# Re-ordering VectorE's stream in a fused two-layer gated cross-attention and mixture-of-experts kernel: an early zeroing of the values' tile, and four moved steps

## The chip, the cores and the metric

The kernel runs on one core of a Trainium2 chip. The metric is the device time in microseconds of one execution. A core has a matrix engine (TensorE, "PE" in the profile), VectorE ("DVE"), ScalarE ("ACT"), GpSimd ("POOL") and a queue engine (SyncE, "SP"), each with an instruction stream of its own that runs in order; streams meet only at semaphores, which this kernel sets and waits for by hand.

## The reference

The state x is 16 sequences of 128 tokens and 128 features, all in fp32. Two layers, each an attention over a context of 77 keys per sequence followed by an expert block:

```
x = x + tanh(g_xattn[0]) * single_head_attention(layernorm(x), ctx)
x = x + tanh(g_ffn[0])   * moe(layernorm(x), 16 experts, top 4, sigmoid gates, one shared expert)
x = x + tanh(g_xattn[1]) * attention_16_heads_of_8(layernorm(x), ctx, Wq, Wk, Wv, Wo and biases)
x = x + tanh(g_ffn[1])   * moe(layernorm(x), 8 experts, top 2, softmax gates)
# an expert: (silu(x @ Wgate) * (x @ Wup)) @ Wdown, weighted by the token's gate
```

## The kernel before, in words

The 16 sequences are four groups g of four tiles t (128 tokens each); a group's tokens are the 512 columns of most operations. The kernel has four stages, here A (first attention), B (first expert block, object `mB`), C (16-head attention), D (second expert block, object `mD`). All orders are written out by hand, engine by engine.

**Start.** SP issues the loads of x, group by group, between other loads. GpSimd zeroes or fills seven small tiles, signals `built` after `qq` (L332), and goes on to zero `VS` (L333), a staging tile for the values of stage C. VectorE waits for `built` and then for the first group of x, and takes its layer-norm statistics (`norm_statsA`, L1069). GpSimd raises the variance to the power -0.5 (`inv_stdA`), VectorE applies it (`norm_applyA`).

**Stages A to B.** The keys of stage C are computed late in stage A: TensorE makes them for one group (`setup_keys`), ScalarE writes the high part, VectorE the low part (`keys_lo(g)`, L1122, semaphore `k_l`). TensorE waits for `k_l` of 3, which is `keys_lo(2)`, before it enters the expert loop of stage B (L663). `VX`, the tile from which stage C's values are multiplied, holds zeroes outside of the copied blocks; GpSimd clears all of it once (L379), after the square root of group 1 (`inv_std(NG + 2)`, L378) and before it splits the shared expert's second matrix `W2S`.

**Expert blocks.** A group has eight units k. For unit k TensorE makes gate and up parts (`m_up`, three passes of a split fp32 product each, L542), ScalarE applies silu into `sg`, VectorE multiplies by the up part (`m_gated`, L1195), then by the token's expert weights (`m_weighted`, L1200), and TensorE multiplies by the down matrix (`m_down`, L564). TensorE runs `m_up(k + 2)` ahead of `m_down(k)`, and `m_up(k)` waits for `m_gated(k - 2)`. The expert weights come through DRAM: the gates are turned on TensorE (`m_route_T`), copied by ScalarE to `ct`, written to `comb_rows`, and read back, broadcast over partitions, into a ring `CR` of four slots (SP, `weight_rows`, L294). Between the units VectorE also does the next group's layer norm (`norm_apply`, L1054; `norm_lo`, L1063) and its routing: `route_add`, `route_vals`, `route_top` (L1147), `route_pick` (L1154), `route_weights` (L1170). In stage B unit 1 is followed by the shared expert's `hs` product (L1223).

**Stage C.** For tile n, TensorE makes the scores (L689), VectorE takes maxima and subtracts them (`c_max`, `c_center`), ScalarE exponentiates, TensorE transposes the probabilities (L699), ScalarE copies them out, TensorE mixes the values (`c_mix`, L713), VectorE divides by the sums (`c_normalize`, L1346), TensorE turns (`c_turn`, L722) and projects (`c_project`, L727), and VectorE adds to x (`c_final`, L1358). `c_turn(n - 2)` and `c_mix(n - 1)` stand in TensorE's stream in the middle of tile n. In the last group stage D's first routing is laid between the tiles.

Of the kernel before, what the change touches and what calls it, by code (L numbers as in the profile page):

```python
# [79 lines left out]
def flamingo(nc, x, ctxT, ctx, w0, w4, gate_router, w13, w2, up, down, consts, out, comb_rows):  # L80
    with ExitStack() as stack:
# [18 lines left out]
        def sem(name):  # L100
            return stack.enter_context(nc.semaphore(name))
# [9 lines left out]
        VX = sb("VX", [P, 2, NC, P])  # L111
# [105 lines left out]
            "c_sc", "c_mx", "c_sub", "c_exp", "c_tr", "c_ev", "c_pv", "c_rs", "c_norm", "c_ot", "c_otc", "c_wo",  # L217
            "c_fin"))
        vs_zero, vx_rdy, wo_rdy = sem("vs_zero"), sem("vx_rdy"), sem("wo_rdy")
        sh_up, sh_silu, sh_hid, sh_hi, sh_lo = map(sem, ("sh_up", "sh_silu", "sh_hid", "sh_hi", "sh_lo"))  # L220
# [104 lines left out]
        def _(pool):  # L325
# [52 lines left out]
            inv_std(NG + 2)  # L378
            nc.gpsimd.memset(VX[:], 0.0)  # L379
            pool.wait_ge(in_w2, 16)  # L380
# [651 lines left out]
        def _(dve):  # L1032
            V = nc.vector
# [178 lines left out]

            def m_body(m, g, nxt, then=None, stats_of=None, apply_next=True, begun=0):

                for k in range(m.units):
                    if k >= begun:
                        m_gated(m, g, k)
                    m_weighted(m, g, k)
                    if then:
# [27 lines left out]
                if then:  # L1247
                    then(m.units)

            dve.wait_ge(in_x[0], 16)  # L1250
            norm_statsA(1, 0)
# [50 lines left out]
            m = mB  # L1302
            m_gated(m, 0, 0)
            norm_apply(NG + 2, 1)
            keys_lo(2)
            m_gated(m, 0, 1)
# [59 lines left out]
            def c_body(g, last):  # L1366
                for t in range(GB):
# [6 lines left out]
                    if ahead:  # L1374
                        c_max(*divmod(n + 1, GB), 0)
                        c_center(*divmod(n + 1, GB), 0)
                    else:
                        route_weights(mD, 0)
                    if n >= 2:
# [8 lines left out]
                    if t == 1 and last:  # L1388
                        route_add(mD, 0)
                    if t == 2 and last:  # L1390
                        route_top(mD, 0)
                        route_pick(mD, 0)
                    if t == 2 and not last:
# [17 lines left out]
            m = mD  # L1411
            m_gated(m, 0, 0)
            c_final(NG - 1, GB - 2)
            c_normalize(NG - 1, GB - 1)
            c_final(NG - 1, GB - 1)


            norm_apply(3 * NG + 2, 1)
            for g in range(NG - 1):
                m_body(m, g, (3 * NG + g + 2, m, g + 1), stats_of=g + 2 if g + 2 < NG else None,  # L1420
                       begun=0 if g else 1)
            m_body(m, NG - 1, None)
# [55 lines left out]
```

## Time and profile before

| | us |
|---|---|
| median of 3 runs | 310.07 |
| the three runs | 307.72, 310.07, 310.26 |
| the profiled execution, device time | 309.45 |
| its span in the profile | 307.6 |
| TensorE busy in it | 278.5 (91%) |
| VectorE busy | 235.0 (76%) |
| ScalarE busy | 130.8 (43%) |
| GpSimd busy | 87.6 (28%) |

The profiled execution has 1.85 us around its span that the profile does not show. The busy time of TensorE is that of modelled ends, so 91% does not mean that it can't be shortened. The granted clock of TensorE averages 0.988 of full speed.

### The profile page before, as it was taken

Reading aid. Unit: us, or ns where it says so; the run is one execution under the profiler, and the core shown is the slowest. Engines: PE = TensorE matmul, PEld = TensorE weight load, DVE = VectorE, ACT = ScalarE, POOL = GpSimd, SP = SyncE. Lnnn points to the kernel's source line nnn. Section 1 sums busy time; section 2 is a strip of 40 time slices with the busy share of each in tenths; the row PEclk is TensorE's granted clock in tenths of the full one; section 3 lists DMA queues with packets and bytes.
Section 4 is the critical chain, followed back from the end, with each engine's and each line's share of the span. In section 5 each row is a group of like instructions: output and inputs, shape, how many; then the busy total and the mean of one; then the engine's idle time right before and its main releaser. Section 6 shows DMA issues by size and latency. Waiting matters only on the chain.

```text
span 307.6 us, 5453 instructions
## 1 busy us (share of the span) xinstructions
PE 278.5 (91%) x1646; PEld 209.3 (68%) x1646; DVE 235.0 (76%) x660; ACT 130.8 (43%) x275; POOL 87.6 (28%) x162
## 2 busy tenths in 40 slices
PE   6799869988999979969989899899899999999994
PEld 5589547666656646637878788789767676676661
DVE  2887879947888998787977977887568869777572
ACT  1497623242234323276656556464622332422330
POOL 8376130100082041452555654751110100100000
PEclk9999979997999999999999999999999999999999
DMA  6900056163143243000000000000043051430640
GB/s 216 351 39 1 4 199 183 52 211 114 41 140 131 48 148 120 26 0 2 2 1 2 0 2 3 0 2 1 6 155 116 29 210 39 153 107 19 233 145 34
DMA packets 15066, 25.26 MB, mean 82 GB/s; under 512 B 2341, under 2 KB 4339, under 8 KB 14835
## 3 DMA queue, kind: packets, MB, share of 16 engines
q1 hardware_dynamic: 12968, 23.88, 23.8%
q10 hardware_dynamic: 2072, 1.07, 1.3%
q8 instruction: 13, 0.21, 0.3%
q14 instruction: 13, 0.11, 0.1%
HBM read 22.98 MB, written 1.25 MB: 79 GB/s over the span
## 4 chain that ended last, share of the span: by engine, by line
PE 67%; DVE 9%; DMA 8%; ACT 5%; issue 4%; POOL 4%; SPq 2%; POOLq 0%; DVEq 0%; ACTq 0%
PE S L542 24%; PE Ybank L564 15%; PE Ybank L713 9%; DMA CR<-comb_rows 4%; PE bank L699 4%; PE S L689 3%; ACT pt L976 2%; DMA comb_rows<-ct 2%; PE Tb L482 2%; DMA X<-in_x 2%; DVE cmx L1334 1%; SPq L307 1%; PE bank L580 1%; POOL KT L354 1%; DVE xn L1059 1%
## 5 line engine op out<-in xcount | busy, mean ns | idle before, releaser
L861 ACT ACTIVATE sg<-S 128x512 f32<-128x512 f32 x64 | 38.1, 597 | 75.4 <-PE S L542 67.2
L1205 DVE TENSOR_TENSOR hb<-sg,CR 128x512 f32<-128x512 f32 x64 | 44.6, 697 | 15.0 <-issue 5.9
L1198 DVE TENSOR_TENSOR sg<-sg,S 128x512 f32<-128x512 f32 x64 | 43.5, 680 | 3.4 <-PE S L542 2.1
L337 POOL TENSOR_TENSOR rstd<-ve,mhalf 128x4 f32<-128x4 f32 x11 | 11.1, 1011 | 111.5 <-DVE ve L1052 111.5
L713 PE MATMUL Ybank<-VX,pt 128*128 128x128 f32 (+1 forms) x320 | 39.7, 275 | 0.0
L542 PE MATMUL S<-xh,WBH 128*128 128x512 f32 x64 | 34.6, 540 | 5.1 <-DVE kk L1125 2.7
L713 PEld LDWEIGHTS Ybank<-VX,pt 128*128 128x128 f32 (+1 forms) x320 | 37.9, 192 | 0.4
L542 PE MATMUL S<-xh,UPH 128*128 128x512 f32 x64 | 36.1, 564 | 0.0
L564 PE MATMUL Ybank<-hb,downw 128*128 128x512 f32 x64 | 33.0, 599 | 0.4 <-DVE hb L1205 0.4
L564 PE MATMUL Ybank<-hb,W2T 128*128 128x512 f32 x64 | 33.1, 602 | 0.0
L1334 DVE TENSOR_REDUCE cmx<-S 128x8 f32<-128x616 f32 x32 | 25.4, 794 | 4.6 <-PE S L689 4.3
L418 POOL COPY VX<-VS 128x36 f32 (+3 forms) x80 | 13.7, 220 | 47.5 <-PE Ybank L713 39.7
L1342 DVE TENSOR_TENSOR PX<-S,cmx 128x616 f32<-128x616 f32 x32 | 25.6, 799 | 1.1
L966 ACT ACTIVATE PX<-PX 128x616 f32<-128x616 f32 x32 | 22.7, 712 | 8.7 <-DVE PX L1342 8.7
L542 PE MATMUL S<-xl,WBH 128*128 128x512 f32 x64 | 26.0, 405 | 0.0
L542 PE MATMUL S<-xh,WBL 128*128 128x512 f32 x64 | 25.9, 405 | 0.0
L542 PE MATMUL S<-xh,UPL 128*128 128x512 f32 x64 | 25.2, 394 | 0.0
L542 PE MATMUL S<-xl,UPH 128*128 128x512 f32 x64 | 25.0, 391 | 0.0
L976 ACT ACTIVATE pt<-bank 128x512 f32<-128x512 f32 (+1 forms) x32 | 15.7, 490 | 18.1 <-PE bank L699 17.9
L542 PEld LDWEIGHTS S<-xh,WBH 128*128 128x128 f32 x64 | 12.6, 196 | 15.0 <-DVE sg L1198 6.7
L354 POOL TENSOR_TENSOR KT<-kk,CB 128x616 fp32r<-128x616 f32 x16 | 19.7, 1234 | 5.8 <-PE S L689 5.8
L699 PE MATMUL bank<-CB,PX 128*128 128x128 f32 x96 | 16.9, 285 | 3.0 <-ACT pt L976 3.0
(164 smaller groups left out, 502.9 us busy)
## 6 DMA issues: line engine op xcount, KB each, us to landing
CR<-comb_rows SPq DMA_DIRECT2D x64, 128.0 KB, 3.1
CR<-comb_rows SPq DMA_DIRECT2D x32, 256.0 KB, 3.3
w13raw<-in_w SPq DMA_DIRECT2D x1, 1088.0 KB, 11.0
X<-in_x SPq DMA_DIRECT2D x4, 256.0 KB, 6.2
upraw<-in_up SPq DMA_DIRECT2D x4, 256.0 KB, 4.0
out_x<-X SPq DMA_DIRECT2D x4, 256.0 KB, 3.3
cT<-in_ctxT SPq DMA_DIRECT2D x2, 308.0 KB, 5.6
CN<-in_ctx SPq DMA_DIRECT2D x1, 616.0 KB
```

Of the source, the lines that this page charges most:

```text
L354: nc.gpsimd.tensor_tensor(KT[:, par].rearrange("p a (h k) -> p a h k", h=HG), keys, heads, ALU.mult).then_inc(ks_done, 1)
L542: i = mm(dst, wp[:, col:col + P], xp[:, bass.ds(xs, GT)], start=n == 0, stop=n == 2)
L564: mm(Ybank[:, bass.ds(slot(g), GT)], m.wd[:, k, :], hb[:, k % 2, :], start=k == 0, stop=k == m.units - 1, skip_group_check=True).then_inc( ...
L699: i = tr(bP[r][0:w, c % 4 * P:c % 4 * P + P], PX[:, t % 2, chunk_col(c):chunk_col(c) + w], I)
L713: i = mm(bO9[u], pt[0:w, t % 2, c * P:(c + 1) * P], VX[0:w, t % 2, c, :], start=c % CU == 0, stop=c % CU == CU - 1)
L861: A(sg[:, k % 2, :], Gb[k % 2][:], ACT.Silu).then_inc(m.s_done, 1)
L966: A(p, p, ACT.Exp).then_inc(c_exp, 1)
L976: A(pt[:, t % 2, 4 * r * P:4 * r * P + w], bPa[r][:, 0:w], ACT.Copy).then_inc(c_ev, 1)
L1198: V.tensor_tensor(sg[:, k % 2, :], sg[:, k % 2, :], Ub[k % 2][:], ALU.mult).then_inc(m.t2, 1)
L1205: V.tensor_tensor(hb[:, k % 2, :], sg[:, k % 2, :], CR[:, k % RING, :], ALU.mult).then_inc(m.h_done, 1)
L1334: V.tensor_reduce(cmx[:, 2 * u:2 * u + 2, :], pair(u), AX, ALU.max, negate=True).then_inc(c_mx, 1)
L1342: V.tensor_tensor(PX[:, t % 2, u * UK:(u + 1) * UK].rearrange("p (s h k) -> p s h k", s=2, h=HG), pair(u), cmx[:, 2 * u:2 * u + 2, :].unsq ...
```

## The change

VectorE, not GpSimd, zeroes `VX`, as its first instruction of all; GpSimd waits for that at the old place. `keys_lo(2)` stands ahead of `norm_apply` of group 1. In stage C `route_top` and `route_pick` of stage D's first group move from behind tile 14's work to behind `c_normalize` of tile 13 in the next step, right ahead of `route_weights`. At the entry of stage D the first `m_weighted` and the second `m_gated` stand ahead of the last `c_final`, where they stood behind it and behind `norm_apply`; `m_body` gets a parameter to leave the first weighted product out.

```diff
@@ gpsimd
             inv_std(NG + 2)
-            nc.gpsimd.memset(VX[:], 0.0)
+            pool.wait_ge(vx_zero, 1)
             pool.wait_ge(in_w2, 16)
@@ vector
-            def m_body(m, g, nxt, then=None, stats_of=None, apply_next=True, begun=0):
+            def m_body(m, g, nxt, then=None, stats_of=None, apply_next=True, begun=0, weighted=0):
                 for k in range(m.units):
                     if k >= begun:
                         m_gated(m, g, k)
-                    m_weighted(m, g, k)
+                    if k >= weighted:
+                        m_weighted(m, g, k)
@@
+            V.memset(VX[:], 0.0).then_inc(vx_zero, 1)
             dve.wait_ge(in_x[0], 16)
             norm_statsA(1, 0)
@@
             m_gated(m, 0, 0)
+            keys_lo(2)
             norm_apply(NG + 2, 1)
-            keys_lo(2)
             m_gated(m, 0, 1)
@@ c_body
                     if ahead:
                         c_max(*divmod(n + 1, GB), 0)
                         c_center(*divmod(n + 1, GB), 0)
                     else:
+                        route_top(mD, 0)
+                        route_pick(mD, 0)
                         route_weights(mD, 0)
@@
                     if t == 1 and last:
                         route_add(mD, 0)
-                    if t == 2 and last:
-                        route_top(mD, 0)
-                        route_pick(mD, 0)
@@
             m_gated(m, 0, 0)
             c_final(NG - 1, GB - 2)
             c_normalize(NG - 1, GB - 1)
+            m_weighted(m, 0, 0)
+            m_gated(m, 0, 1)
             c_final(NG - 1, GB - 1)
             norm_apply(3 * NG + 2, 1)
             for g in range(NG - 1):
                 m_body(m, g, (3 * NG + g + 2, m, g + 1), stats_of=g + 2 if g + 2 < NG else None,
-                       begun=0 if g else 1)
+                       begun=0 if g else 2, weighted=0 if g else 1)
```

## Rows read from the trace of the kernel before

**Rows 1.** The page: the chain that ended last, shares by engine

```profile
PE 67%; DVE 9%; DMA 8%; ACT 5%; issue 4%; POOL 4%; SPq 2%; POOLq 0%; DVEq 0%; ACTq 0%
```

**Rows 2.** The chain in order of time, 38 to 48 us: start, duration, what

```profile
38.36 2.44 DVE xn L1059 x4
...
41.39 2.92 PE S L542 x6
...
46.47 1.39 PE S L542 x6
```

**Rows 3.** Timeline, first 9 us: start, duration, what, count, idle before and releaser

```profile
2.40 3.70 POOL L333 MEMSET VS<- 128x4320 f32 x1
...
5.00 0.87 DVE L1074 BATCH_NORM_STATS2 st<-X 128x6 f32<-128x128 f32 x4 [5.00 <-DMA X<-in_x]
...
7.24 0.87 DVE L1074 BATCH_NORM_STATS2 st<-X 128x6 f32<-128x128 f32 x4 [0.45 <-DMA X<-in_x]
```

**Rows 4.** Timeline, 37 to 48 us, from stage A into B

```profile
37.77 0.68 DVE L1198 TENSOR_TENSOR sg<-sg,S 128x512 f32<-128x512 f32 x1
...
38.01 2.23 POOL L379 MEMSET VX<- 128x2560 f32 x1
...
41.39 0.79 PE L542 MATMUL S<-xh,WBH 128*128 128x512 f32 x1 [2.67 <-DVE kk L1125]
...
41.86 1.28 DVE L1205 TENSOR_TENSOR hb<-sg,CR 128x512 f32<-128x512 f32 x2
...
45.84 0.68 DVE L1223 TENSOR_TENSOR hs<-hs,bank 64x512 f32<-64x512 f32 x1 [2.25 <-ACT hs L898]
...
46.46 0.69 DVE L1065 TENSOR_TENSOR xl<-Tb,xh 128x512 fp32r<-128x512 f32 x1
...
47.70 0.18 PE L588 MATMUL Tb<-GW,xh 128*128 128x32 f32 x1
```

**Rows 5.** Line 1059's instructions: min, median and max ns, first and last start

```profile
L1059 DVE TENSOR_SCALAR xn<-X,mv,rstd x28: 328/343/1956, 38.4 to 264.5; 128x128 f32<-128x128 f32 x20, 128x128 f32 x8
```

**Rows 6.** The two ring loads issued at 38.5 and 39.1 us (slot 1): their landing

```profile
DMA to landing us min/median/max: 3.1/3.2/3.2
```

**Rows 7.** Stretches: length, each engine's busy time, TensorE's granted clock, DMA

```profile
41.50:42.00 0.50, 0.50 (x2) 0.41 (x3) 0.50 (x2) 0.00 (x0) 0.00 (x0) 0.50 0.66 238
...
73.00:74.00 1.00, 1.00 (x4) 0.89 (x4) 0.42 (x1) 0.00 (x0) 0.00 (x0) 0.50 0.54 193
...
217.00:218.00 1.00, 0.92 (x8) 0.92 (x9) 0.25 (x3) 0.51 (x3) 0.00 (x0) 1.00 0.00 0
```

**Rows 8.** Timeline, 213 to 220 us, the last tiles of stage C

```profile
213.05 2.40 PE L713 MATMUL Ybank<-VX,pt 128*128 128x128 f32 x20
...
215.06 0.39 DVE L1151 MAX8 top<-valsD 128x8 f32<-128x14 f32 x4
...
216.46 0.25 DVE L1352 RECIPROCAL rec<-Ybank 128x16 f32<-128x16 f32 x1
...
217.09 0.33 PE L722 MATMUL Tb<-CB,On 128*128 128x128 f32 x1 [1.20 <-DVE On L1355]
...
218.33 0.29 DVE L1364 TENSOR_TENSOR X<-Tb,X 128x128 f32<-128x128 f32 x1
...
219.24 0.27 PE L594 MATMUL Tb<-CB,combD 128*32 128x128 f32 x1
```

**Rows 9.** Landing of stage D's first ring load (issued at 221.84); of all ring loads

```profile
DMA to landing us min/median/max: 3.4/3.4/3.4
...
DMA to landing us min/median/max: 2.7/3.2/5.2
```

**Rows 10.** Timeline, 225 to 230 us, entry of stage D

```profile
225.12 0.29 DVE L1355 TENSOR_TENSOR On<-Ybank,rec 128x128 f32<-128x128 f32 x1
...
228.20 0.68 DVE L1205 TENSOR_TENSOR hb<-sg,CR 128x512 f32<-128x512 f32 x1
...
229.03 1.10 PE L564 MATMUL Ybank<-hb,downw 128*128 128x512 f32 x2
```

More of the change, by code:

```diff
@@ L218, in flamingo @@
             "c_fin"))
+        vx_zero = sem("vx_zero")
         vs_zero, vx_rdy, wo_rdy = sem("vs_zero"), sem("vx_rdy"), sem("wo_rdy")
```

## The prediction

> **What bounds the kernel now.** I read the page's chain of work first: two thirds of the span are TensorE's own instructions, one behind the other, and a tenth is VectorE's [rows 1]. So only what removes or shortens a wait of TensorE, or of the chain that hands over to it, can count; the reader should look for the places where the chain leaves TensorE. Then the chain in order of time, which shows one such place at 38 us: a `norm_apply` of 2.44 us on VectorE, and TensorE's six passes behind it, 2.92 us where the same six take 1.39 later [rows 2]. Then the timelines around the four edits, and for each idle time the engine that ended it [rows 3, 4, 8, 10].
>
> **The zeroing leaves GpSimd (stage A to B).** The four `xn` instructions of `norm_apply` start at 38.36; the row of their line gives a median of 343 ns and one of 1,956 ns [rows 5]. The long one is the first of the four: it starts inside the GpSimd zeroing, which runs 38.01 + 2.23 = 40.24 [rows 4], and 38.36 + 1.96 = 40.32. It is held until GpSimd has finished. With the zeroing gone, 1.96 - 0.34 = 1.6 us leave VectorE's stream. What comes to stand there on GpSimd is the short split of `W2S`, which could hold the first `xn` by some tenths; I charge 0.1 to 0.2 within the roundings below. The Trainium skill, page "SBUF — State Buffer", section "Who interferes with whom", names this: a VectorE operation in a two-port mode, such as tensor_scalar, and a GpSimd operation exclude each other for the whole instruction, and the later one blocks. By it the `W2S` split, if issued first, would hold `xn` until its own end; the sum stays.
>
> **keys_lo(2) ahead of norm_apply.** TensorE stands idle 2.67 us until 41.39, for `keys_lo(2)` [rows 4]. In the new order that follows the gated product of 37.77 (next start some 0.61 later, 38.4) and takes at most what a 512-column operation takes, 0.69 [rows 4]: done by 39.0. TensorE enters the expert loop at 39.0, 2.4 sooner. I don't count that 2.4, but follow the chain to the next point where both orders meet, the logits of the next group, which begin at 47.70 [rows 4]:
> - VectorE: `norm_apply` to 40.0, second gated product to 40.7, first weighted product to 41.4. The second weighted product needs ring slot 1, whose second half is issued at 39.1 and lands 3.2 later, at 42.3 [rows 6]. Before, it started at 41.86 + 0.6 = 42.5 [rows 4]. So VectorE meets a transfer here, and all its lead shrinks to 0.2. It goes on: product to 42.9, `keys_lo(3)` to 43.4.
> - Then VectorE before stood idle 2.25 us for ScalarE's shared-expert silu, until 45.84 [rows 4], which waited for TensorE. TensorE now makes: 39.0, six passes 1.4 [rows 2], three for the shared expert 0.7, the turn of `xn` about 0.5, to 41.6; so ScalarE has its input at 41.1 and is not behind 43.4 by more than a tenth or two, with three operations of some 0.6 after 41.4. The `hs` product starts at 43.4 to 43.5, 2.4 sooner, and `xl`, before at 46.46, ends at 44.7 rather than 47.15.
> - TensorE: down product at 41.6, six passes by 43.5, then it waits for `xl` until 44.75. Logits at 44.75 rather than 47.70: **2.9 us**. Should the clock fall as before (the granted clock was 0.50, of its two levels 1.2 GHz, right after the idle time [rows 7]) in the first six passes, they take 2.9 instead of 1.4, and TensorE arrives at about 44.8 to 45: hardly a loss, since `xl` ends last.
>
> Does the 2.9 last? VectorE is ahead by 2.4 only, so 0.5 less than TensorE; from here on TensorE sets the pace (its passes follow without idle time in the chain), and I take VectorE's reserve as larger than 0.5. The next group's weights leave for DRAM behind TensorE's turn and come back through the ring; nothing there waits for an absolute time, so the whole lead goes through stage B. Bounds: 1.9 (the `xn` is still long, see the rivals) to 3.6 (with full clock and a slot landing sooner).
>
> **The zeroing comes to VectorE's start.** VectorE has no zeroing in the trace, so I bound it. From 128 to 512 columns two VectorE rows grow from 0.29 [rows 10] to 0.68 [rows 4], 1.02 ns a column, so 2,560 columns cost 2.6 + 0.16 = 2.8 us; at 0.68 / 512 all in, 3.4; GpSimd's own rate gives 2.23. I take 2.8, from rows of the same engine. The Trainium skill, page "VectorE: DVE Perf Modes", section "Zero memsets can be issued as uint32 (trn2)", gives one cycle an element, from which an estimate at its 0.96 GHz is 2.7 us. GpSimd frees VectorE when `VS` starts, 2.40 [rows 3], plus a tenth or two for VectorE's own semaphore steps: the zeroing ends at 5.3 to 5.4, at most 6.0. VectorE's first statistics start at 5.00, but before the second set it is idle 0.45 until the load lands at 7.24 [rows 3]. So an end up to 5.45 is free, and beyond that it costs one for one: **0 to 0.55, taken as 0.1**. GpSimd's wait at the old place is for something done 30 us before: nothing.
>
> **Routing picks in the last tile of stage C.** `route_top` to the end of `route_pick` fill 215.06 to 216.46, and `c_normalize` begins then, although its input, the mix of 213.05 + 2.40 = 215.45, is ready 1.0 sooner; TensorE's turn waits 1.20 us for it, to 217.09 [rows 8]. Reversed, `c_normalize` (0.25 + 0.29 [rows 8, 10]) runs from 215.5, and the turn comes at about 216.1. What is late next: the picks end at 217.4, `route_weights` at about 218.0, `c_final` at 218.3; before, `c_final` began at 218.33 and `m_route_T` at 219.24 [rows 8]. Moved by 1.0, TensorE would reach `m_route_T` at 218.25 and finds `c_final` just done: 0.9 remains. ScalarE's tanh now waits for the picks between two copies and delays a copy by 0.2, which only a mix four microseconds on uses. **Gain 0.9**, bounds 0.5 to 1.0.
>
> **The entry of stage D.** The first weighted product needs the first ring load, issued at 221.84 and landed 3.4 later, at 225.24 [rows 9]; VectorE reaches it at 225.12 + 0.29 = 225.4 [rows 10]. Both move together by 0.9. So it costs 0.6 in a time when VectorE waited for TensorE's last projection, and the gated product too. `norm_apply` comes no later. Then the down product no longer follows a product begun at 228.20, but the turn: it starts at about 228.9 instead of 229.03 [rows 10], and the next passes save some hundredths. **Gain 0.2**, bounds 0.4 and a loss of 1.6 (rivals).
>
> **Sum.** -2.9 + 0.1 - 0.9 - 0.2 = -3.9 against the profiled execution: 309.45 - 3.9 = 305.55 (span 303.7). That execution lies 0.62 below the median of the runs; the median of all four executions shown (307.72, 309.45, 310.07, 310.26) is 309.76, and from that I forecast 305.9.
>
> **Rivals.**
> - *The clock takes part of it back.* TensorE gets a new idle time of 1.2 us (43.5 to 44.75). In stage B an idle time came before a second stretch at 0.50 of the clock, at 73 us; the 1.20 us in stage C was followed by full clock, at 217 us [rows 7, 8]. Should it fall for 3.2 us, 1.6 are lost: -2.3, 307.5. Chance 0.12.
> - *VectorE's zeroing is held at the start by GpSimd's `VS`*, as the `xn` was by `VX`. `VS` ends at 6.10 [rows 3], the zeroing then at 8.9, 3.4 beyond the free 5.45: net -0.5, 309.3. Against it: the statistics of 5.00 ran beside `VS` in 0.87, as the undisturbed ones did at 7.24 [rows 3]. The skill's SBUF section above exempts a VectorE instruction with at most one SBUF input outside the two-port modes, and so lowers this chance. Chance 0.06.
> - *Slower than before*: the same hold, and with it TensorE's clock. It idles 3.4 us longer in stage A, more than the 2.67 that came before the fall to 0.50 [rows 4, 7], and loses 1.6 to slow passes: 3.9 against 5.0, 310.9. It decides from the point where the zeroing ends later than 5.45 + 3.9 = 9.35. Chance 0.05, of which little lies over 1%.
> - *The first ring load of stage D lands late.* At 5.2, the longest landing of a ring load [rows 9], VectorE holds the last `c_final` and `norm_apply` by 1.6: -2.3, 307.5. Chance 0.07.
> - *The long `xn` had another cause* and stays: then only `keys_lo(2)` gains, and the logits come 1.9 sooner: -2.9, 306.9. Chance 0.05.
>
> **How the numbers follow.** The forecast as told has 0.65. Its own spread is the bounds, 304 to 307.5. The range takes in the clock, the late load and half of the hold: 303.8 to 309.2. About 1% (3.1 us) is what a measurement of this kernel can tell from no change. Faster by more: most of the forecast's case and part of the last rival, 0.65; within 1%: the clock, the late load, the hold, and the forecast's lower edge, 0.30; slower by more, 0.05.
>
> **What would show it.** No instruction of line 1059 at 38 us above 0.4; TensorE's wait for `kk` below 0.5 in place of 2.67, and a new one for `xl` of about 1.2 just before the logits; VectorE's wait for ScalarE before `hs` gone and a short one for the ring before the second `hb`. At the start a zeroing of 2.7 to 2.8 on VectorE, and the second statistics still at 7.24. In the last tile of stage C the turn's idle time near 0.2. At the entry of stage D no wait before the first `hb`. The prediction is wrong if the second statistics start late, if the clock reads 0.5 after 44 us, or if the lead of 2.9 at the logits has shrunk where the next group's weights are written.

## The result, and the profile after

The changed kernel takes 303.22 us, the median of 6 runs (302.62 to 303.55); the kernel before took 307.58 beside it (median of 6, 305.13 to 310.26; three of the six are the runs that the forecast was made from). The ratio is 0.987 [0.984, 0.990]: 1.3% faster. The forecast was 305.9 (range 303.8 to 309.2), a gain of 3.9 us or 1.26%. The gain between the medians is 4.4 us, and the time itself lies 0.6 us below the range.

The profiled execution of the changed kernel took 303.55 us (span 301.7, mean granted clock 0.993) against 309.45 (span 307.6, clock 0.988): 5.9 us less, more than the medians differ. The page, first its engines, then the shares of the chain that ended last (compare [rows 1]):

```profile
PE 277.1 (92%) x1646; PEld 208.5 (69%) x1646; DVE 236.2 (78%) x661; ACT 130.8 (43%) x275; POOL 85.5 (28%) x161
...
PE 70%; DVE 8%; DMA 6%; ACT 5%; POOL 4%; issue 4%; SPq 0%; POOLq 0%; DVEq 0%; ACTq 0%
```

TensorE has 70% of the chain instead of 67%: waits went, and its work stayed.

**The start.** Timeline of the changed kernel, first 9 us (compare [rows 3]):

```profile
2.40 3.70 POOL L334 MEMSET VS<- 128x4320 f32 x1
...
3.64 2.19 DVE L1252 MEMSET VX<- 128x2560 f32 x1 [3.64 <-issue]
...
5.75 0.81 DVE L1075 BATCH_NORM_STATS2 st<-X 128x6 f32<-128x128 f32 x4
...
7.39 0.87 DVE L1075 BATCH_NORM_STATS2 st<-X 128x6 f32<-128x128 f32 x4
```

The zeroing's row is 2.19 us long, not 2.8 (how long it holds VectorE, f2 below shows); it starts at 3.64, later than forecast, and ends at 5.83. The first statistics move from 5.00 to 5.75, the second from 7.24 to 7.39. `VS` beside it on GpSimd lasts 3.70, as before.

**Stage A to B.** Timeline of the changed kernel, 37 to 46 us (compare [rows 4]):

```profile
37.91 0.67 DVE L1199 TENSOR_TENSOR sg<-sg,S 128x512 f32<-128x512 f32 x1
...
38.15 0.29 POOL L382 CAST W2S<-W2T 128x128 fp32r<-128x128 f32 x1
...
39.12 0.54 DVE L1126 SCALAR_TENSOR_TENSOR kk<-bank,CB,kk 128x308 fp32r<-128x308 f32 x1 [0.54 <-ACT kk L856]
39.58 1.11 DVE L1060 TENSOR_SCALAR xn<-X,mv,rstd 128x128 f32<-128x128 f32 x4
...
42.33 0.69 DVE L1206 TENSOR_TENSOR hb<-sg,CR 128x512 f32<-128x512 f32 x1 [0.45 <-DMA CR<-comb_rows]
...
43.99 0.68 DVE L1066 TENSOR_TENSOR xl<-Tb,xh 128x512 fp32r<-128x512 f32 x1
...
45.07 0.18 PE L589 MATMUL Tb<-GW,xh 128*128 128x32 f32 x1
```

`norm_apply` fell from 2.53 (2.44 of it in the chain) to 1.11. The second weighted product waits 0.45 for its ring load, the new wait that the prediction named. The logits (the product with `GW`, L588 before, L589 here) start at 45.07 instead of 47.70, 2.63 sooner (forecast 2.9). The wait before `hs` is gone.

The chain in order of time, same kernel (compare [rows 2]), and under it stretches of it: length, busy time of each engine with its instructions, then granted clock, DMA share and GB/s (compare [rows 7]):

```profile
34.91 2.81 PE S L543 x6
38.53 1.40 PE S L543 x6
...
43.84 1.39 PE S L543 x6
```

```profile
36.00:38.00 2.00, 2.00 (x6) 1.46 (x5) 1.81 (x10) 1.11 (x2) 0.82 (x1) 0.50 0.06 16
...
42.00:44.00 2.00, 2.00 (x11) 1.34 (x10) 1.67 (x4) 1.76 (x3) 0.00 (x0) 1.00 0.58 211
72.00:76.00 4.00, 4.00 (x16) 2.63 (x15) 3.55 (x15) 0.69 (x2) 0.00 (x0) 1.00 0.22 77
```

Between 10 and 290 us the clock still falls once, but earlier (34.8 to 38.2 us). The stretch at 0.50 of the kernel before at 71.9 to 75.3 us ([rows 7] has its middle) is not there.

**Stage C's end and the entry of D.** Timeline, 210 to 223 us (compare [rows 8, 10]):

```profile
210.10 0.26 DVE L1355 RECIPROCAL rec<-Ybank 128x16 f32<-128x16 f32 x1 [0.33 <-PE Ybank L714]
...
210.60 0.39 DVE L1152 MAX8 top<-valsD 128x8 f32<-128x14 f32 x4
210.74 0.33 PE L723 MATMUL Tb<-CB,On 128*128 128x128 f32 x1 [0.24 <-DVE On L1358]
...
219.05 0.68 DVE L1206 TENSOR_TENSOR hb<-sg,CR 128x512 f32<-128x512 f32 x1
...
222.63 1.02 PE L565 MATMUL Ybank<-hb,downw 128*128 128x512 f32 x2
```

The turn waits 0.24 instead of 1.20, and the first weighted product of D waits for nothing.

To add up, I cut both profiled executions at events that both have: TensorE's turn that sends group 0's weights off (`m_route_T`), the logits of group 1, the four writes of `comb_rows` in stage B (one for each group, the last three used here), the four in stage D, and the end. Each step is a difference of two starts in a timeline.

| step (us) | before | after | difference | forecast |
|---|---|---|---|---|
| start to the turn | 34.47 | 34.61 | +0.14 | +0.1 |
| turn to logits | 13.23 | 10.46 | -2.77 | -2.9 |
| logits to the write of group 1 | 10.89 | 10.89 | 0 | 0 |
| write of group 1 to that of group 2 | 24.77 | 21.54 | -3.23 | 0 |
| write of group 2 to that of group 3 | 22.45 | 22.94 | +0.49 | 0 |
| write of group 3 to D's first | 114.09 | 113.19 | -0.90 | -0.9 |
| D's first to second write | 21.92 | 21.73 | -0.19 | -0.2 |
| D's second to fourth write | 39.74 | 39.74 | 0 | 0 |
| D's fourth write to the end | 26.07 | 26.63 | +0.56 | 0 |

The column adds up to the 5.9 us between the spans. The four terms of the forecast came out to 0.15. Three other steps moved that it left at nothing. The last, 0.56, is a ring load of the last group: it landed after 3.87 instead of 3.27 us and VectorE waited 3.19 instead of 2.59 for it; f1, a variant of the kernel before, has 3.91 and 3.23 there, so it isn't the change's doing. The 3.23, of which 0.49 comes back in the next step, is what the experiments are about.

### The profile page after: what moved, and what is told of

It reads as the page before. It is cut to its first block, busy times and chain, and to the rows that moved or that the text cites. A ratio compares the mean times of both kernels' runs of the same rounds, so it can differ in the third digit from the quotient of the medians.

```text
span 301.7 us, 5454 instructions
## 1 busy us (share of the span) xinstructions
PE 277.1 (92%) x1646; PEld 208.5 (69%) x1646; DVE 236.2 (78%) x661; ACT 130.8 (43%) x275; POOL 85.5 (28%) x161
## 4 chain that ended last, share of the span: by engine, by line
PE 70%; DVE 8%; DMA 6%; ACT 5%; POOL 4%; issue 4%; SPq 0%; POOLq 0%; DVEq 0%; ACTq 0%
PE S L543 25%; PE Ybank L565 15%; PE Ybank L714 10%; DMA CR<-comb_rows 4%; PE bank L700 4%; PE S L690 3%; ACT pt L977 2%; DMA comb_rows<-ct 2%; PE Tb L483 2%; POOL KT L355 1%; PE bank L581 1%; DVE xn L1060 1%; PE Tb L728 1%; POOL xn L405 1%; DVE cmx L1337 1%
## 5 line engine op out<-in xcount | busy, mean ns | idle before, releaser
L543 PE MATMUL S<-xh,WBH 128*128 128x512 f32 x64 | 33.8, 529 | 3.1 <-DVE sg L1199 3.0
L967 ACT ACTIVATE PX<-PX 128x616 f32<-128x616 f32 x32 | 22.7, 712 | 8.7 <-DVE PX L1345 8.7
L977 ACT ACTIVATE pt<-bank 128x512 f32<-128x512 f32 (+1 forms) x32 | 15.7, 489 | 18.1 <-PE bank L700 17.9
```

The costliest lines, as they stand in the source:

```text
L543: i = mm(dst, wp[:, col:col + P], xp[:, bass.ds(xs, GT)], start=n == 0, stop=n == 2)
L967: A(p, p, ACT.Exp).then_inc(c_exp, 1)
L977: A(pt[:, t % 2, 4 * r * P:4 * r * P + w], bPa[r][:, 0:w], ACT.Copy).then_inc(c_ev, 1)
```

## The experiments

Each was timed beside the kernel before and profiled. Time is the median with its range and number of executions, then the ratio to before with its 95% interval.

**The parts by themselves.** Four kernels make one edit each in the kernel before, one makes the first two; the changed kernel ran again beside them.

```diff
 e1_zero_alone
-            nc.gpsimd.memset(VX[:], 0.0)
+            pool.wait_ge(vx_zero, 1)
...
+            V.memset(VX[:], 0.0).then_inc(vx_zero, 1)
             dve.wait_ge(in_x[0], 16)
 e2_keys_alone
+            keys_lo(2)
             norm_apply(NG + 2, 1)
-            keys_lo(2)
 e3_picks_alone
                     else:
+                        route_top(mD, 0)
+                        route_pick(mD, 0)
                         route_weights(mD, 0)
...
-                    if t == 2 and last:
-                        route_top(mD, 0)
-                        route_pick(mD, 0)
 e4_entry_alone
             c_normalize(NG - 1, GB - 1)
+            m_weighted(m, 0, 0)
+            m_gated(m, 0, 1)
             c_final(NG - 1, GB - 1)
```

> Only the zeroing moves to VectorE's start. Theory 1 (the held norm_apply is the root of the 2.9 us, and keys_lo(2) would follow early enough by itself): TensorE's wait for keys_lo(2) shrinks from 2.67 to about 1.2 us, the logits of group 1 come some 2.5 us sooner than before, and the time falls by 2.3 to 2.8 us (ratio near 0.992). Theory 2 (the order of keys_lo(2) is what pays): the time falls by under 1 us. Either way the start costs 0.15 us.

> Only keys_lo(2) moves ahead of norm_apply; GpSimd still zeroes VX beside it, so one xn instruction stays at nearly 2 us. Theory 1: the logits come 1.9 us sooner, time -1.5 to -2. Theory 2: -2.5 or more.

> Only the routing picks of stage D's first group move behind c_normalize. TensorE's idle time before the turn of tile 13 falls from 1.20 us to 0.24, and the time by 0.9 us (ratio 0.997). A rival, that the path to the first ring load takes it back: under 0.3.

> Only the first weighted product and the second gated product move ahead of the last c_final. Expected -0.1 to -0.2 us, not to be told from nothing; the rival, a late ring load, would show as idle time before the first hb of stage D and cost up to 1.6 us.

> The zeroing and keys_lo(2) moved, stages C and D as before. Theory 1: logits of group 1 some 2.6 us sooner, time -2.5 to -3. Should a second fall of TensorE's clock in stage B be what makes slow executions of the kernel before, and be gone here, the executions of this kernel will scatter by under 1 us where those of before scatter by up to 5, and the median falls by up to 3.5.

> The whole change again, on the chip of the next two kernels, to compare them with: ratio to before 0.985 to 0.99.

Measured (steps from each one's profiled execution; the last column says where the granted clock was 0.50 between 10 and 290 us):

| kernel | time | ratio | turn to logits | group 1's to group 2's write | group 3's write to D's first | clock at 0.50, us |
|---|---|---|---|---|---|---|
| before | | | 13.23 | 24.77 | 114.09 | 41.1-44.5, 71.9-75.3 |
| e1, zeroing | 304.81 (304.28-306.15, 12) | 0.992 [0.989, 0.995] | 10.53 | 21.55 | 114.10 | none |
| e2, keys | 304.68 (303.99-305.47, 12) | 0.993 [0.991, 0.996] | 10.43 | 21.78 | 114.07 | none |
| e3, picks | 306.01 (304.67-308.04, 12) | 0.995 [0.992, 0.999] | 13.24 | 21.89 | 113.19 | 12.3-15.7, 43.0-46.4 |
| e4, entry | 306.81 (304.90-308.60, 12) | 0.999 [0.996, 1.003] | 11.79 | 24.67 | 114.07 | 70.6-74.0 |
| e5, zeroing and keys | 304.60 (304.08-306.36, 12) | 0.992 [0.989, 0.994] | 10.56 | 21.73 | 114.13 | 34.8-38.2, 130.3-133.8 |
| changed, again | 303.69 (303.09-304.52, 6) | 0.988 [0.984, 0.993] | 10.04 | 21.70 | 113.60 | 129.5-132.9 |

Two things follow. First, the two edits of stage A and B are for the most part substitutes. e1 gains 2.4 us and e2 2.5, so neither of the two theories on record, each with one edit as the root, is right alone, and e5 with both gains 2.7. In the step, either gives 10.4 to 10.5 without a fall of the clock; both together give 10.4 to 10.6 with a fall at 35 us (changed, e5, and e6 and f4 below) and 10.04 to 10.41 without one (changed again, and f2, f3 and g3 below). The timelines of e1 and e2 show why:

```profile
39.68 1.25 DVE L1060 TENSOR_SCALAR xn<-X,mv,rstd 128x128 f32<-128x128 f32 x4
...
40.85 0.53 DVE L1126 SCALAR_TENSOR_TENSOR kk<-bank,CB,kk 128x308 fp32r<-128x308 f32 x1
...
43.77 0.69 DVE L1206 TENSOR_TENSOR hb<-sg,CR 128x512 f32<-128x512 f32 x1 [0.79 <-DMA CR<-comb_rows]
```

```profile
38.66 0.53 DVE L1125 SCALAR_TENSOR_TENSOR kk<-bank,CB,kk 128x308 fp32r<-128x308 f32 x1
39.11 2.08 DVE L1059 TENSOR_SCALAR xn<-X,mv,rstd 128x128 f32<-128x128 f32 x4
...
41.71 1.37 DVE L1205 TENSOR_TENSOR hb<-sg,CR 128x512 f32<-128x512 f32 x2
```

In e1 (upper fence) VectorE gets 1.2 us from the shorter `norm_apply` and gives 0.79 back to a ring load. In e2 (lower) the `norm_apply` is still held, 2.08, but TensorE no longer waits for it, and the products fall just behind the landing. Whoever frees VectorE meets the same ring loads.

Second, the old order gives two different values, 13.23 or 13.24 with a stretch at 0.50 there (before and e3, each behind an idle time of 2.67) and 11.79 without one (e4, and twice more below). So of the 2.8 us of this step in the two profiles, 1.3 are the order and 1.45 are a clock fall that this execution of the kernel before had and others have not. (Without a fall in either the order is worth more, 11.79 against 10.04 to 10.41.) The table's next column shows a fall too: 24.67 and 24.77 with one near 71 us, 21.5 to 21.9 without; more on it below, where executions without one have 22.5 (h3), 22.7 (f3) and 23.2 (e7).

E3's step of 113.19 and E4's of stage D (21.70 against 21.92 before) are the forecast's third and fourth term, each by its own edit: 0.9 and 0.2. e4's median can't tell its 0.2 from nothing.

**Another way to free VectorE's start.** The zeroing on GpSimd, but ahead of `inv_std(NG + 2)`, where it meets no `norm_apply`; the second also moves `inv_std(NG + 4)` behind `split_up`. Both keep the other edits.

```diff
             split_w13(4)
+            nc.gpsimd.memset(VX[:], 0.0)
             inv_std(NG + 2)
-            pool.wait_ge(vx_zero, 1)
...
-            V.memset(VX[:], 0.0).then_inc(vx_zero, 1)
 e7_pool_early_split, besides
-            inv_std(NG + 4)
...
+            inv_std(NG + 4)
```

> The whole change, but GpSimd zeroes VX, ahead of the square root of group 1, where it stood idle for 8.26 us before; VectorE's start has no zeroing. If where the zeroing collides is all that matters, this gives all that the whole change gives, and the 0.15 us of the start as well: no xn above 0.4 us at 38 us, and a time 0 to 0.3 us below the whole change's. If VectorE's start costs more than the trace shows, it gives more.

> As the kernel before it, and GpSimd splits the up matrices between the square roots of groups 2 and 3 of stage B, not after both, where a norm_apply of VectorE ran 2.65 us beside it in place of 1.1. If the hold between the two engines is the rule, that norm_apply falls to about 1.1 us, TensorE's idle time of 1.38 us behind it goes, and the time falls by 1 to 1.4 us more. If the split then holds other VectorE instructions on the chain, less or nothing.

e6: 304.42 (303.52 to 306.73, 12), 0.991 [0.988, 0.994]; e7: 304.75 (303.30 to 306.75, 12), 0.992 [0.988, 0.995]; neither beats the changed kernel's 303.69. e6 was expected at or up to 0.3 us below it and lies 0.7 above; its `norm_apply` takes 1.10 as it should and its profiled execution took 303.63, so where the 0.7 comes from is not shown. e7 removed a long `norm_apply` in stage B as meant. First the changed kernel, then e7:

```profile
80.92 2.65 DVE L1060 TENSOR_SCALAR xn<-X,mv,rstd 128x128 f32 x4
```

```profile
71.54 1.52 POOL L390 TENSOR_TENSOR UPL<-upraw,UPH 128x512 fp32r<-128x512 f32 x1 [0.18 <-POOL UPH L388]
71.83 1.28 DVE L1142 TENSOR_SCALAR score<-score 128x64 f32<-128x64 f32 x1
...
87.32 0.69 DVE L1205 TENSOR_TENSOR hb<-sg,CR 128x512 f32<-128x512 f32 x1 [2.26 <-DMA CR<-comb_rows]
```

The `norm_apply` at 83.35 took 1.11, but VectorE then waits 2.26 for the ring, and the step from group 1's to group 2's write takes 23.16 instead of 21.54. The reason is that the split, moved to 66 to 75 us, holds other VectorE instructions there. A `score` of 64 columns lasts 1.28 instead of 0.19. The hold is moved, not removed: it now stands in the routing, whose weights the ring then brings late. The Trainium skill, page "SBUF — State Buffer", section "Who interferes with whom", says that a VectorE operation in a two-port mode, such as `tensor_scalar`, and a GpSimd operation exclude each other for the whole instruction and that the later one blocks. These rows agree: 71.83 + 1.28 = 73.11 is just behind the split's 71.54 + 1.52 = 73.06.

**Is it TensorE's idle time that makes the clock fall?** The kernel before with nine passes that nothing reads, put into its idle time of 2.67 us:

```diff
 (in the kernel before, PE, behind setup_keys(3))
+            pe.wait_ge(route["rdy"], 1)
+            for n in range(9):
+                mm(Tb[:], WBH[:, 0:P], xh[:, 0:GT], start=True, stop=True)
```

> The kernel before, with nine more fp32r passes of TensorE (128x512, result in a free bank, read by nobody) in the idle time of 2.67 us before keys_lo(2) is seen. They add work and no result. Theory C (part of the median's gain is that the change keeps TensorE's clock up, since the idle time in stage B makes it fall): no stretch at 0.50 from 41 us on, the executions below 0.9975 of mean clock get rarer, and the median falls from about 307.3 towards the 306.0 of the executions of before at full clock, by 0.5 to 1.3 us. Rival (the falls come for another reason, earlier or at random): no change within 0.3 us, and the mean clocks as mixed as before.

306.71 (305.62 to 308.77, 12), 0.998 [0.996, 1.001]. Timelines of f1 and then of e4, whose idle time is not filled:

```profile
38.83 2.46 PE L665 MATMUL Tb<-xh,WBH 128*128 128x512 f32 x9
...
41.90 0.50 PE L542 MATMUL S<-xh,WBH 128*128 128x512 f32 x1 [0.61 <-DVE kk L1128]
...
46.75 0.18 PE L588 MATMUL Tb<-GW,xh 128*128 128x32 f32 x1
```

```profile
41.43 0.50 PE L542 MATMUL S<-xh,WBH 128*128 128x512 f32 x1 [2.65 <-DVE kk L1125]
...
46.29 0.18 PE L588 MATMUL Tb<-GW,xh 128*128 128x32 f32 x1
```

And stretches of e4 (f1's clock is 1.00 from 42 to 43 as well):

```profile
42.00:43.00 1.00, 1.00 (x6) 0.83 (x5) 1.00 (x2) 0.34 (x1) 0.00 (x0) 1.00 0.72 232
71.00:72.00 1.00, 1.00 (x6) 0.90 (x5) 0.09 (x1) 0.00 (x0) 0.00 (x0) 0.50 0.58 98
```

f1 had no fall at 41 us and its step is 11.79; but e4 idled 2.65 us, had no fall either, and its step is 11.79 too. So the run decides nothing about this place: an idle time of 2.65 does not always bring a fall, and filling it gained nothing that the times show. Nor do the mean clocks: 4 of f1's 12 executions have 0.9975 or more, beside 24 of 127 of the kernel before. At 71 us both did fall, which is taken up below.

**Doubling the zeroing.** The changed kernel with a second zeroing of the same size at VectorE's start (of `pt`), which nothing needs; beside it the changed kernel without the entry's edit, and the changed kernel again.

```diff
 f2_more_zeroing
+            V.memset(pt[:], 0.0)
             V.memset(VX[:], 0.0).then_inc(vx_zero, 1)
 f3_no_entry
             c_normalize(NG - 1, GB - 1)
-            m_weighted(m, 0, 0)
-            m_gated(m, 0, 1)
             c_final(NG - 1, GB - 1)
```

> The whole change, with a second zeroing of 2,560 columns (of the tile pt, which is written anew later) ahead of VectorE's first. Theory: VectorE's start has about 0.3 us of room and the zeroing takes 2.2 us, so this costs 2.0 to 2.3 us in full, ratio to before near 0.996. If the chip has more room at the start than the trace shows, under 1 us. If GpSimd's zeroing of VS holds it or is held by it, VectorE's first zeroing lasts beyond 2.3 us or ends with VS at 6.1.

> The whole change without its last part (first weighted and second gated product of stage D stay behind norm_apply). Forecast for that part: 0.2 us, so the median 0.1 to 0.3 above the whole change's. From the executions of its part alone at full clock (305.2 against 306.0) it could be 0.8.

> The whole change, on the chip of the three kernels before it: median about 3.6 to 4.3 us below before's, and its executions within 1.5 us of each other whatever their mean clock.

f2: 307.92 (306.83 to 310.15, 12), 1.003 [1.000, 1.006]; f4: 304.65 (303.49 to 305.48, 6), 0.991 [0.987, 0.994]. So a second zeroing costs 3.3 us, more than the expected 2.0 to 2.3. Timeline of f2:

```profile
3.64 2.19 DVE L1252 MEMSET pt<- 128x2560 f32 x1 [3.64 <-issue]
6.31 2.19 DVE L1253 MEMSET VX<- 128x2560 f32 x1 [0.48 <-issue]
8.42 0.81 DVE L1075 BATCH_NORM_STATS2 st<-X 128x6 f32<-128x128 f32 x4
```

The second row starts 2.67 after the first, and the statistics start 2.67 later than in the changed kernel (8.42 - 5.75). So 2.67 us, 1.04 ns a column, is what a zeroing takes out of VectorE's time here; its row shows 2.19 of that, and the other 0.48 the profile puts to "issue". In this execution TensorE's granted clock is 0.50 from 12.1 to 18.9 us, and the turn comes at 39.66 instead of 34.61. That looks like the mechanism of the rival "slower than before", late statistics and then slow passes. The mean clocks of all twelve executions, 0.981 to 0.994, fit it, but e3 had a fall at 12.3 us without late statistics, so the fall's cause is not shown.

f3: 304.79 (304.06 to 305.81, 6), 0.992 [0.989, 0.995], 0.14 above f4; the medians can't tell 0.2 from nothing, but the step's length shows it (21.93 against 21.74 in f4).

**The ring load that now ends last: one transfer for a slot instead of two.** Each slot's two loads of 64 partitions are made one of 128, in the changed kernel (g1) and in the kernel before (g2); g3 is the changed kernel again. Besides what is shown, the counts that VectorE waits for are halved, and TensorE waits once for the load of the down matrices.

```diff
-                    for e in range(m.per):
-                        n = P // m.per
-                        sp.dma_start(CR[e * n:(e + 1) * n, k % RING, :],
-                                     at[m.per * k + e:m.per * k + e + 1, :].to_broadcast([n, GT])).then_inc(
-                                         ring_in[k % RING], 16)
+                    n = P // m.per
+                    sp.dma_start(CR[:, k % RING, :],
+                                 at[m.per * k:m.per * k + m.per, :].unsqueeze(1).to_broadcast([m.per, n, GT])).then_inc(
+                                     ring_in[k % RING], 16)
```

> The whole change, and each ring slot of stage B is filled by one load over 128 partitions instead of two over 64 (TensorE waits once for the load of the down matrices, which is long in). SP then issues slot 1 about 0.6 to 1.2 us sooner. If it is that landing at which the lead of VectorE ends after the change (0.45 us of idle time before the second hb, and the same lead for either edit alone), the logits of group 1 come up to 0.6 us sooner, until TensorE itself is late, and each later group's wait for its first loads shortens too: -1 to -3 us in all. If a single load of 256 KB lands later by as much as its issue is saved, nothing.

> The same single loads in the kernel before. Its second hb never waited for the ring at 42 us, so the logits of group 1 stay; what it gains comes from the later groups alone, so less than the kernel with the change gains, by about 0.5 us.

> The whole change on the same chip as the two: 3.6 to 4.3 us below before. At most one full stretch at half clock between 30 and 100 us in the profile costs time here; from the last ring wait to the write of group 2's weights 21.5 to 21.8 us without one and 23.9 or more with one.

g1: 405.28 (404.36 to 406.85, 6), 1.317 [1.311, 1.323]; g2: 406.48 (405.81 to 408.29, 6), 1.321 [1.315, 1.327]; g3: 303.52 (303.25 to 304.85, 6), 0.987 [0.982, 0.991]. A hundred microseconds slower, where one to three were to be gained. Timeline of g1 and a stretch of it (same columns as above), and under them the like stretch of the changed kernel:

```profile
45.48 0.69 DVE L1206 TENSOR_TENSOR hb<-sg,CR 128x512 f32<-128x512 f32 x1 [4.47 <-DMA CR<-comb_rows]
...
50.75 0.69 DVE L1206 TENSOR_TENSOR hb<-sg,CR 128x512 f32<-128x512 f32 x1 [4.57 <-DMA CR<-comb_rows]
```

```profile
42.00:44.00 2.00, 0.22 (x2) 0.00 (x0) 0.00 (x0) 0.00 (x0) 0.00 (x0) 1.00 0.13 49
```

```profile
40.00:42.00 2.00, 2.00 (x10) 1.59 (x9) 1.88 (x5) 0.54 (x2) 0.00 (x0) 1.00 0.62 195
```

The products come 5.27 apart, each waiting for its load. The mean share of the 16 DMA engines is 0.13, that of two engines (2/16 = 0.125), at 49 GB/s, against 0.62 and 195 GB/s. The pattern's slowest dimension is now the two experts. The Trainium skill, page "DMA: Bandwidth & Descriptors", section "Rules for kernel authors", has a rule for it: a transfer whose outermost dimension has a size c under 16 is confined to at most c engines. These rows agree with it. The order of the dimensions was not varied by itself.

**Is it slot 1's loads alone?** ScalarE issues slot 1's two loads behind its first silu instead of SyncE behind slot 0's, for group 0 of stage B (h1, and h3 in the kernel before) or for every group (h2).

```diff
-                    for e in range(m.per):
+                    for e in range(0 if m is mB and g == 0 and k == 1 else m.per):
...
+            def ring_one(g):
+                act.wait_ge(rows_out, 16 * (g + 1))
...
+                for e in range(2):
+                    act.dma_start(CR[e * 64:(e + 1) * 64, 1, :],
+                                  comb_rows[g][2 + e:3 + e, :].to_broadcast([64, GT])).then_inc(ring_in[1], 16)
```

> The whole change, and ScalarE issues the two loads of ring slot 1 for the first group, behind its first silu, where it stood idle; SP goes from slot 0 to slot 2. They start about a microsecond sooner and should land at about 41.3 instead of 42.3 us. If that landing cuts the lead, the second hb starts at about 41.9 without idle time, xl ends 0.4 us sooner and the logits of group 1 come 0.1 to 0.5 us sooner (TensorE's own passes are next). If the lead is cut elsewhere, the idle time before the second hb goes and the logits stay.

> As the kernel before, for all four groups of stage B: ScalarE issues slot 1 once the weights are in DRAM, ahead of its second silu. VectorE's wait before the second hb of group 1 (1.35 us) should go; TensorE's wait there is only 0.4 to 0.5 us, so -0.4 to -1.0 us against the whole change's 303.5, with fewer long idle times before the clock can fall.

> The kernel before with ScalarE's loads of slot 1 for the first group alone. Its second hb met no wait for the ring, since the held norm_apply came later; so nothing: within 0.5 us of before. If it gains over 1 us, the ring bound the kernel before as well.

h1: 305.42 (303.43 to 306.43, 12), 0.994 [0.991, 0.998]; h2: 304.06 (303.26 to 306.99, 12), 0.992 [0.988, 0.995]; h3: 306.46 (305.79 to 309.98, 12), 1.001 [0.997, 1.005]. No gain, and turn to logits is 10.71 in h1 (10.0 to 10.5 in the changed kernel) and 11.79 in h3. h1:

```profile
37.85 1.42 ACTq L945 DMA_DIRECT2D CR<-comb_rows  x2
...
39.87 0.54 DVE L1136 SCALAR_TENSOR_TENSOR kk<-bank,CB,kk 128x308 fp32r<-128x308 f32 x1 [0.82 <-ACT kk L856]
...
42.29 1.33 DVE L1216 TENSOR_TENSOR hb<-sg,CR 128x512 f32<-128x512 f32 x2 [0.26 <-DMA CR<-comb_rows]
```

The second product no longer waits behind the first (the two are one group of 1.33). But the issue takes ScalarE 1.42, `keys_hi(2)` comes after it, and `keys_lo(2)` waits 0.82 for that. TensorE waits 1.12 for `keys_lo(2)`, where in g3 it waits 0.22. So the gain was paid for on ScalarE, and what remains is a wait of 0.26 before the first product, for slot 0. h1's execution has a fall of the clock at 69.9 us too. In h2 the second product of group 1 no longer waits (0.04 instead of 1.35), but the first waits 2.34 instead of 1.47 and TensorE's wait for `xl` is 0.52, so the expected 0.4 to 1.0 didn't come. That the kernel before gains nothing (h3) agrees with its trace: its two products ran without a wait [rows 4]. How much the landing of slot 1 alone is worth in the changed kernel stays partly open.

**Where the 3.2 us up to group 2's write come from: read, not tried.** This step was not in the forecast, so I followed it in the profiled executions. Two rows of the kernel before, then the two that answer to them in the changed one:

```profile
68.26 0.69 DVE L1205 TENSOR_TENSOR hb<-sg,CR 128x512 f32<-128x512 f32 x1 [2.70 <-issue]
...
70.29 0.26 PE L588 MATMUL Tb<-GW,xh 128*128 128x32 f32 x1 [1.94 <-DVE xl L1065]
```

```profile
64.08 0.69 DVE L1206 TENSOR_TENSOR hb<-sg,CR 128x512 f32<-128x512 f32 x1 [1.35 <-issue]
...
66.11 0.25 PE L589 MATMUL Tb<-GW,xh 128*128 128x32 f32 x1 [0.38 <-DVE xl L1066]
```

In group 1 too VectorE stands before the product of slot 1; the profile names no releaser, but that slot's second load, issued with the first at 62.45 (59.83 in the changed kernel), lands after 5.2 us before and 3.7 after. TensorE then waits for `xl`, and the clock may fall about two microseconds later (left out are g1 and g2, and h2, where ScalarE issues these loads):

| slot 1's longer landing in group 1, us | kernels | TensorE's wait for `xl` | fall after it (69 to 75 us) |
|---|---|---|---|
| 5.2, 5.2, 4.8 | before, e4, f1 | 1.94, 1.90, 1.46 | all three |
| 4.8, 4.6, 4.6, 4.4 | f3, h1, h3, f4 | 1.52, 1.31, 1.29, 1.12 | h1 and f4 |
| 4.0 | e3 | 0.70 | no |
| 3.5 to 3.9 | changed, e1, e2, e5, changed again (e5's, g3), e6, e7, f2 | 0.21 to 0.61 | none |

So about half of the 3.2 is a wait (1.94 - 0.38 = 1.6) and half a clock fall of some 1.6: h1 and h3, with like waits, take 24.10 with a fall and 22.48 without. Of these 1.6, 1.0 comes back by group 3's write: over both steps h1 and h3 differ by 0.6 only (46.04 and 45.40), and the kernel before and the changed one by 2.74 (47.22 and 44.48). A landing of 4.0 or more stands in all five executions with the old order in stages A and B, and in three of the twelve with either or both of its edits (f3, f4, h1). It may be something that the edits make rarer, by moving the ring loads against the other transfers of that time. No kernel was run that moves only those, and five executions against twelve are few, so this cause is open.

**All executions together.** The kernel before was timed again beside every set of experiments: 127 executions, median 307.28 (quartiles 306.2 and 308.1, range 305.06 to 312.09); the changed kernel has 24, median 303.57 (303.3 and 304.1; 302.62 to 305.48). Sorted by the mean granted clock of each execution:

| mean clock | before | changed |
|---|---|---|
| 0.9975 or more | 305.95 (24 of 127; 305.06-306.72) | 303.57 (6 of 24; 303.25-304.14) |
| less | 307.62 (103) | 303.60 (18) |
| correlation of time and clock | -0.70 | -0.37 |

At full clock the change is worth 2.4 us. Over all executions it is worth 3.7, because the kernel before is another 1.7 slower in its executions with a lower mean clock and the changed kernel is not. This is a sorting, not an experiment: late landings and falls come together in the profiles, and it doesn't part them. The repeats of the changed kernel were expected 3.6 to 4.3 us below before and gave 3.0 (f4) and 4.8 (g3); The executions of e5, which by its theory should have scattered by under 1 us, spread over 2.3, and those of f4, expected within 1.5, over 2.0.

## Why the prediction was right and where it failed

- **VectorE's zeroing at the start** (forecast 2.8 us long, +0.1): right. The row is 2.19 long, but what a zeroing takes of VectorE's time is 2.67 by f2, near the 2.8 of the slope and the 2.7 of the second estimate. What was off is the start: counted back 2.67 from the statistics at 5.75, the zeroing takes VectorE's time from 3.08 on (an estimate), not from 2.5 to 2.6. The second set starts 0.15 later in the two profiles, and over all of them it can't be told: 7.2 to 7.7 without VectorE's zeroing, 7.4 to 7.8 with one. f2 shows that the free room is used up: a second one costs all of its length and more.
- **The long `xn` was GpSimd's hold**: right. It is gone in the changed kernel and in e1, stays in e2 (2.08), and e7's `score` shows the same pair in another place. The line now reads, beside [rows 5]:

```profile
L1060 DVE TENSOR_SCALAR xn<-X,mv,rstd x28: 333/340/1293, 39.6 to 258.1; 128x128 f32<-128x128 f32 x20, 128x128 f32 x8
```

  The 1,293 that is left is not in this place, whose four take 1.11 together.
- **keys_lo(2) and the lead at the logits** (2.9): 2.63 by the start of the logits, 2.77 from the turn. The mechanism was right: the ring's second slot, named as what VectorE meets, makes it wait (0.45), and the logits come 10.04 to 10.56 after the turn, forecast 44.75 - 34.47 = 10.28. The term was mis-sized by its origin: 1.3 of it is the order, or up to 1.75 where neither execution has a fall, and 1.45 is the slow stretch of the profiled execution, which e4, f1 and h3 with the same old order don't have. And most of the order's gain comes from either edit alone (e1, e2). A fall is "hardly a loss" in the new order, as forecast: 10.46 and 10.41 with one at 35 us, 10.04, 10.12 and 10.41 without, against 1.45 in the old order.
- **The new idle time of 1.2 us before the logits**: mostly not there. In the changed kernel's profile the passes at 34.91 took 2.81, so TensorE arrived late. In its two repeats without a fall at this place (e5's and g3) the wait is 0.25 and 0.20. g3 shows the step that was missed: the down product, forecast at 41.6, waits for the first weighted product, and that one for slot 0's load, 0.55:

```profile
41.22 0.69 DVE L1206 TENSOR_TENSOR hb<-sg,CR 128x512 f32<-128x512 f32 x1 [0.55 <-DMA CR<-comb_rows]
...
42.06 1.10 PE L565 MATMUL Ybank<-hb,W2T 128*128 128x512 f32 x2 [0.17 <-DVE hb L1206]
...
44.75 0.25 PE L589 MATMUL Tb<-GW,xh 128*128 128x32 f32 x1 [0.20 <-DVE xl L1066]
```

  So the rival built on this idle time (the clock takes part back) had no ground here. A wait for `xl` of that size does come in the next group, in some executions, and there a fall came behind it in h1 (1.31) and f4 (1.12).
- **"The whole lead goes through stage B"**: it was kept, and 3.2 more came between the writes of groups 1 and 2, of which 0.5 went back before that of group 3. "Nothing there waits for an absolute time" left out the ring's landings, which differ from execution to execution: 5.2 against 3.7 for one load of group 1, a wait of TensorE behind it, and the second clock fall behind that. This is most of why the two profiles differ by 5.9 and the medians by 3.7 to 4.4.
- **Routing picks** (0.9, bounds 0.5 to 1.0): 0.90, in the changed kernel and in e3 alone; the changed kernel's turn waits 0.24.
- **Entry of stage D** (0.2): 0.19 to 0.22 in the steps of e4 and the changed kernel; too little for the medians. No late load came.
- **Rivals.** The hold by `VS` is refuted: the zeroing ran inside `VS`, 2.19 beside 3.70, the latter as before. "Slower than before" did not come; with the start 2.7 late f2 is slower than the changed kernel by 3.3 and level with the kernel before. "The long `xn` had another cause" is refuted by e1 and e2.
- **The step that failed: how the profiled execution stands to the median.** The base of 309.76, to which the gain was applied, was taken from four executions. Three of the four lie above 308.1, where only a quarter of all 127 do, whose median is 307.28. With 307.3 the same gain of 3.9 gives 303.4, beside 303.2 to 303.7 measured (f4: 304.65). The range was built from bounds of the gain alone, and the base had none, although the four spread over 2.5 us, nearly as much as the gain. By that median the base was 2.5 too high, more than the 0.6 by which it misses the range.
- **What was luck in the size.** By the steps the edits are worth -1.3 + 0.15 - 0.9 - 0.2 = -2.25 us without the slow stretch of the kernel before (-2.65 with 1.7 for the first term, where the changed kernel has none either), beside 2.4 at full clock. The forecast's 3.9 held another 1.45 of slow clock out of one execution. The medians hold about 1.3 more than 2.4 too, but as a mean over many executions: 103 of the kernel before's 127 have a mean clock under 0.9975 and take 1.7 longer, and the changed kernel's time doesn't show its falls. One place says why: a fall at 35 us delays the logits by 0.4 at most. For the others it is not shown. That the forecast's 3.9 lies between the medians' 3.7 and 4.4 is luck to that extent.

## What to carry to other kernels

Before an idle time of an execution is booked as a gain, ask whether the slow stretch beside it belongs to the kernel or to that execution: take the same step, and the landings in it, out of several executions, and give the base a spread of its own. Two edits that free the same engine ahead of the same transfer are substitutes, so follow each to the next thing that doesn't move, and don't add them. A GpSimd operation that holds VectorE is only worth moving to where VectorE runs nothing of the kind, and each new place has its own neighbours.

## What the runs showed of the hardware

- A VectorE zeroing of 128x2560 fp32 has a row of 2.19 us, also beside a GpSimd zeroing, and takes 2.67 us of VectorE's time: two of them start 2.67 apart, with 0.48 between the rows (f2). VectorE's first row starts at 3.64 us, TensorE's, released by the same GpSimd signal, at 2.52.
- A load whose outermost dimension is 2 showed the DMA share of two of the 16 DMA engines (0.13, 49 GB/s): one came every 5.3 us, and the whole kernel took 1.32 times as long (g1).
- A VectorE `tensor_scalar` of 128x64 beside a GpSimd `tensor_tensor` of 1.52 us lasted 1.28 us instead of 0.19 and ended with it (e7).
- The granted clock falls to 0.50 (1.2 of the two levels, 1.2 and 2.4 GHz), in some executions of a program and not in others; the falls of the kernel before lasted 3.4 us each. In group 1 of stage B one came in five of the seven tabled executions in which TensorE had waited 1.12 to 1.94 us, and in none of the ten in which it had waited 0.21 to 0.70; at the entry of stage B an idle time of 2.65 to 2.67 had a fall beside it in the kernel before and e3 and none in e4 and h3. What decides it was not found.
- The same 128 KB ring load landed after 3.5 us in one execution (e1) and after 5.2 in another (before).
- Two loads issued by ScalarE took 1.42 us of its time, and its next operation had 1.73 us of idle time before it (h1).
